# Probabilities turned by VectorE block transposes and DMAs across partitions, in place of TensorE transposes

## The reference: what is computed

```python
# first branch: 16 heads of 64, causal
q, k, v = einsum('bse,ef->bsf', xn, W_qkv)           # (8, 512, 3, 16, 64)
q, k = rotary_embedding(q), rotary_embedding(k)
scores = einsum('bqhd,bkhd->bhqk', q, k) / 8
weights = softmax(where(tril, scores, -1e9))
attn = einsum('bhqk,bkhd->bqhd', weights, v).reshape(8, 512, 1024) @ W_out
# second branch: 16 heads of 8, not causal, then a mixture of 8 experts
q, k, v = xn @ Wq + bq, xn @ Wk + bk, xn @ Wv + bv
ctx = softmax(q k^T / sqrt(8)) v
y = xn + layernorm(ctx @ Wo + bo)
p = softmax(y @ Wg + bg);  top 2 of 8 experts, weighted
ffn = y + layernorm(sum of the two picked (y @ We[e] + bexp[e]) * p[e])
out = x + attn + ffn
```

## Time and profile before

| what | before |
|---|---|
| median of three runs | 1271.35 us (1267.77 to 1273.54) |
| profiled execution: its span | 1270.3 us |
| instructions | 25325 |
| busy PE / DVE / ACT / POOL | 1159.3 / 928.0 / 892.0 / 811.5 us |
| mean granted TensorE clock | 0.978 |
| DMA traffic | 42.87 MB, 34 GB/s |

### The profile page before, as it was taken

One profiled execution on the slowest core, in us unless ns is written; L12 is line 12 of the kernel. 1 busy time (PEld: TensorE's weight loads), 2 busy tenths in 40 slices (PEclk: granted clock), 3 DMA queues, 4 the chain that ended last, 5 costly groups with the idle time before them and its releaser, 6 DMA issues.

```text
span 1270.3 us, 25325 instructions
## 1 busy us (share of the span) xinstructions
PE 1159.3 (91%) x9387; PEld 741.3 (58%) x9387; DVE 928.0 (73%) x2336; ACT 892.0 (70%) x1841; POOL 811.5 (64%) x730
## 2 busy tenths in 40 slices
PE   4779999999999999999999999999999999899986
PEld 3355565655666565655656556665656556575655
DVE  7666487885878857896687848787687866778546
ACT  3567867487766868578775887668776796748860
POOL 3655774577855767568864778467675587645760
PEclk8799999999999999999999999999999999999998
DMA  4000100011000110001100011001000011000000
GB/s 144 34 34 18 43 35 17 26 39 38 34 18 26 51 43 26 18 26 59 39 13 35 26 43 42 18 26 51 34 29 24 25 35 51 18 17 34 34 18 9
DMA packets 34110, 42.87 MB, mean 34 GB/s; under 512 B 5694, under 2 KB 17216, under 8 KB 33988
## 3 DMA queue, kind: packets, MB, share of 16 engines
q1 hardware_dynamic: 30516, 38.31, 8.2%
q10 hardware_dynamic: 3472, 2.95, 0.8%
HBM read 5.60 MB, written 2.10 MB: 6 GB/s over the span
## 4 chain that ended last, share of the span: by engine, by line
PE 59%; DVE 17%; ACT 14%; issue 4%; POOL 4%; DMA 1%; SPq 0%; ACTq 0%; DVEq 0%; POOLq 0%
PE work L1319 7%; PE work L1233 7%; PE work L1334 6%; PE work L1346 6%; PE work L1235 6%; PE work L1234 6%; PE work L1396 5%; DVE fnmax L1071 5%; ACT fpt L884 5%; PE work L1362 4%; ACT pn L926 4%; DVE work L1193 3%; PE work L1371 3%; PE work L1386 3%; ACT pt L938 2%
## 5 line engine op out<-in xcount | busy, mean ns | idle before, releaser
L926 ACT ACTIVATE pn<-work,nmax 128x512 f32<-128x512 f32 (+3 forms) x512 | 265.3, 534 | 119.9 <-DVE nmax L1193 119.4
L785 POOL TENSOR_TENSOR raw<-raw,cos_t 128x512 f32<-128x512 f32 x128 | 163.8, 1280 | 284.9 <-DMA swapped<-raw 269.7
L1071 DVE TENSOR_REDUCE fnmax<-work 128x2 f32<-128x1024 f32 x256 | 302.0, 1219 | 47.0 <-PE work L1371 45.8
L1193 DVE CUSTOM_DVE_ANT_0 work<-work,causal 128x512 f32<-128x512 f32 (+3 forms) x512 | 236.1, 520 | 95.5 <-PE work L1319 94.7
L884 ACT ACTIVATE fpt<-work 128x1024 f32<-128x1024 f32 x256 | 252.4, 1029 | 52.7 <-PE work L1386 51.4
L1334 PE MATMUL work<-consts,pn 128*128 128x128 f32 x1280 | 172.6, 277 | 7.0 <-DVE fnmax L1071 4.0
L789 POOL TENSOR_TENSOR raw<-raw,swapped 128x512 f32<-128x512 f32 x128 | 163.7, 1279 | 10.0
L1334 PEld LDWEIGHTS work<-consts,pn 128*128 128x128 f32 x1280 | 141.1, 141 | 42.7 <-DVE fnmax L1071 13.0
L800 POOL TENSOR_TENSOR qk_l<-raw,qk_h 128x512 fp32r<-128x512 f32 x128 | 163.3, 1282 | 2.8
L786 POOL TENSOR_TENSOR swapped<-swapped,sin_t 128x512 f32<-128x512 f32 x128 | 163.7, 1279 | 0.0
L938 ACT COPY pt<-work 128x1024 f32<-128x1024 f32 x128 | 130.4, 1019 | 42.6 <-PE work L1334 42.1
(11 more groups left out here) (161 smaller groups left out, 2140.1 us busy)
## 6 DMA issues: line engine op xcount, KB each, us to landing
swapped<-raw SPq DMA_DIRECT2D x256, 128.0 KB, 2.0
x_in<-in_L_attn_x_dram SPq DMA_DIRECT2D x8, 256.0 KB, 3.4
out_dram<-x_in SPq DMA_DIRECT2D x7, 256.0 KB, 2.2
fpt<-in_L_attn_W_qkv_dram ACTq DMA_DIRECT2D x3, 512.0 KB, 5.9
pt<-in_L_ffn_We_dram ACTq DMA_DIRECT2D x1, 512.0 KB, 7.2
wout<-in_L_attn_W_out_dram ACTq DMA_DIRECT2D x1, 512.0 KB, 8.4
out_dram<-x_in SPq DMA_DIRECT2D x2, 128.0 KB, 1.8
pt<-in_rope_dram ACTq DMA_DIRECT2D x1, 192.0 KB, 6.5
```

What stands on the lines that cost most here:

```text
L785: nc.gpsimd.tensor_tensor(raw[:, n % 3], raw[:, n % 3], cos_t[:], ALU.mult)
L926: ins = nc.scalar.activation(pn[:, h, PN_AT[j]:PN_AT[j] + n], bank_of(("sc", b, c, unit), h)[:, at:at + n], ACT.Exp, scale=-1.0, bias=nmax ...
L1071: nc.vector.tensor_reduce(fnmax[:, j, 2 * r:2 * r + 2, 0:1], bank_of(("fsm", b, g, j), 2 * r, 2).rearrange("p (f n) -> p f n", f=2), AX.X, ...
L1193: ins = nc.vector.tensor_tensor_reduce(out=scores, in0=scores, in1=causal[:, S - n:S], scale=-1.0 / math.sqrt(DH), scalar=3.0e38, op0=ALU.add,
```

## The change

What it does, part by part:

1. The transposes `tp`, `tq` and their copies `tpe`, `tqe` go. A new kind `tr` on DVE (line 1588 of the changed kernel) transposes 32 x 32 blocks of `pn` in place, three instructions a chunk: 128 x 8 x 128, 128 x 8 x 128 and 128 x 8 x 64 elements, one for each unit of `exp`. A new kind `shuf` on SP's queue (line 1140) then sends, with four DMAs a chunk, each from 32 partitions of `pn` to all 128 of `pt`, 128 x 640 elements (327,680 bytes), so that blocks which belong to one key land on one partition. `pn` becomes double, `pt` single; `exp` waits for the `shuf` of two chunks ago, `shuf` waits for the third `tr` and for the `pv` of the chunk before, `pv` waits for its `shuf`.
2. A 32 x 32 block transpose would leave keys in another order than tiles of 128 need. So POOL's `hi` and `lo` write keys (k = 1) with a step of 32 elements, the mask is put in the same order once, `exp` writes runs of 32, `pv` reads runs of 32, in five groups of four matmuls instead of four (the same 1280 columns), and the query tiles stand in reverse order in `rT` and `ao`.
3. Second branch: `fqk` is made once a batch with the plain weights (6 matmuls of 128 x 512 instead of 24), `fqkh` and `fqkl` with 2 instructions a batch instead of 8; a new kind `fdup` on SP (line 1147), three DMAs a group, spreads the parts over the strips. `fsub` writes to a buffer of its own, `fqm`, and also waits for the `fst` of the group before.
4. `fan` writes straight to `l_wide` (and so waits for the `div` of the chunk before). At the start a few transposes, casts and small DMAs are fewer, and raw loads stand in `pn` instead of `pt`.
5. The tables START, SHIFT, FIRST, LAST become one table PLACE with a place number for each instance; the PSUM table changes too.

```diff
```diff
+TILES_OF = {3: 0, 2: 4, 0: 7, 1: 8}
+UNIT_TILES = [slice(0, 4), slice(4, 8), slice(8, 10)]
+PT_N = T * (T + 1) // 2
+QUADS = P // STRIP
...
-START = {
-    "turn": [-465.460287],
...
+PLACE = {
+    "xT": [
+        [0],
...
-        pn = sb("pn", [P, 2, PT_N])
-        pt = sb("pt", [P, 2, 2, PT_N])
-        l_rows = sb("l_rows", [P, S])
+        pn = sb("pn", [P, 2, QUADS, 2, PT_N, STRIP])
+        pt = sb("pt", [P, QUADS, 2, PT_N, STRIP])
-        fqk = sb("fqk", [P, 2, 2, S], F32R)
+        fqn = sb("fqn", [P, 4, S], F32R)
+        fqs = sb("fqs", [P, 2, 2, S], F32R)
+        fqm = sb("fqm", [P, S], F32R)
...
+        def landed(kind, *key):
+
+            sems, per, dmas = (fdup_done, G, 3) if kind == "fdup" else (shuf_done, NC, QUADS)
+            n = key[0] * per + key[1]
+            return (sems[n % 2], 16 * dmas * (n // 2 + 1)) if n >= 0 else (begun, 1)
 
...
+                elif kind == "shuf":
+                    c = x_[2]
+                    wait(sp, after("tr", b, c, 2))
+                    wait(sp, after("pv", *ring(1, b, c, NC)))
+                    for a in range(QUADS):
+                        sp.dma_start(pt[:, a].rearrange("p h n r -> p (h n r)"),
+                                     pn[a * STRIP:(a + 1) * STRIP, c % 2].rearrange("p c h n r -> p c (h n r)")).then_inc(shuf_done[c % 2], 16)
+                elif kind == "fdup":
+                    g = x_[2]
+                    wait(sp, after("fqkl", b))
+                    wait(sp, after("fst", *ring(2, b, g, G), T - 1))
+                    for c, pair in ((1, slice(0, 4, 2)), (2, slice(1, 3)), (3, slice(0, 4, 3))):
+                        sp.dma_start(fqs[c:P:4, g % 2].bitcast(F32), fqn[g * STRIP:(g + 1) * STRIP, pair].bitcast(F32))                            .then_inc(fdup_done[g % 2], 16)
...
+            def turned(a, k):
+                return a.rearrange("p (t c r) -> p t r c", c=QUADS, r=STRIP) if k == 1 else a
+            def plain(a, k):
+                return a.rearrange("p (t r c) -> p t r c", c=QUADS, r=STRIP) if k == 1 else a
...
-                    nc.gpsimd.tensor_copy(qk_h[:, c % 2, k], raw[:, n % 3]).then_inc(done["hi"], 1)
+                    nc.gpsimd.tensor_copy(turned(qk_h[:, c % 2, k], k), plain(raw[:, n % 3], k)).then_inc(done["hi"], 1)
...
-                    nc.gpsimd.tensor_tensor(qk_l[:, c % 2, k], raw[:, n % 3], qk_h[:, c % 2, k].bitcast(F32),
-                                            ALU.subtract).then_inc(done["lo"], 1)
+                    nc.gpsimd.tensor_tensor(turned(qk_l[:, c % 2, k], k), plain(raw[:, n % 3], k),
+                                            turned(qk_h[:, c % 2, k].bitcast(F32), k), ALU.subtract).then_inc(done["lo"], 1)
...
                 elif kind == "fqkh":
-                    g = x_[2]
-                    wait(act, after("fst", *ring(2, b, g, G), T - 1))
+                    wait(act, after("fqk", b))
...
+                    for k in range(2):
+                        ins = nc.scalar.activation(fqn[:, 2 * k], bank_of(("fqk", b), k), ACT.Identity, bias=qk_bias[:, k:k + 1])
...
-                        wait(act, after("tp", *ring(1, b, c, NC), 1))
-                        wait(act, after("tq", *ring(1, b, c, NC)))
+                        wait(act, landed("shuf", *ring(2, b, c, NC)))
+                        if b == 0 and c < 2:
+                            for kind_ in LOADED:
+                                wait(act, after(kind_, 0))
...
-                        ins = nc.scalar.activation(pn[:, h, PN_AT[j]:PN_AT[j] + n], bank_of(("sc", b, c, unit), h)[:, at:at + n],
+                        tiles = slice(TILES_OF[j], TILES_OF[j] + j + 1)
+                        ins = nc.scalar.activation(pn[:, c % 2, :, h, tiles].rearrange("p c i r -> p i c r"),
+                                                   bank_of(("sc", b, c, unit), h)[:, at:at + n].rearrange("p (i c r) -> p i c r", r=STRIP, c=QUADS),
...
-                elif kind == "tpe":
-                    c, unit = x_[2:]
...
-                        wait(act, after("pv", *ring(2, b, c, NC)))
-                    nc.scalar.copy(pt[:, c % 2, :, unit * S:(unit + 1) * S],
...
                     wait(act, after("inv", b, c))
-                    wait(act, after("rT", *ring(1, b, c, NC)))
-                    nc.scalar.copy(l_rows[:].rearrange("p (t h n) -> p t h n", t=T, h=2),
+                    wait(act, after("div", *ring(1, b, c, NC)))
+                    nc.scalar.copy(l_wide[:].rearrange("p (t h n) -> p t h n", t=T, h=2),
...
                 elif kind == "fqkl":
-                    g = x_[2]
-                    wait(dve, after("fqkh", b, g))
+                    wait(dve, after("fqkh", b))
...
-                    nc.vector.tensor_tensor(fqk[:, g % 2, 0], bank_of(("fmT", b, g)), fqk[:, g % 2, 0].bitcast(F32),
-                                            ALU.add).then_inc(done["fsub"], 1)
+                    wait(dve, after("fst", *ring(1, b, g, G), T - 1))
+                    nc.vector.tensor_tensor(fqm[:], bank_of(("fmT", b, g)), fqs[:, g % 2, 0].bitcast(F32), ALU.add).then_inc(done["fsub"], 1)
...
-                elif kind == "tqe":
-                    c = x_[2]
-                    wait(dve, after("tq", b, c))
...
+                elif kind == "tr":
+                    c, unit = x_[2:]
+                    wait(dve, after("exp", b, c, unit, 0), after("exp", b, c, unit, 1))
+                    blocks = pn[:, c % 2, :, :, UNIT_TILES[unit]].rearrange("p c h n r -> p c h (n r)")
+                    nc.vector.transpose(blocks, blocks).then_inc(done["tr"], 1)
...
-                    g = x_[2]
-                    if g == 0:
-                        wait(pe, after("xl", b))
-                        if b == 0:
-                            wait(pe, after("strl", 0))
+                    wait(pe, after("xl", b))
+                    if b == 0:
+                        wait(pe, after("strl", 0))
                     for k in range(2):
-                        wh = strips_h[:, k, g * GH:(g + 1) * GH].rearrange("p h c -> p (h c)")
-                        wl = strips_l[:, k, g * GH:(g + 1) * GH].rearrange("p h c -> p (h c)")
-                        ins = split3(bank_of(x_, k), wh, wl, xt_h[:, b % 2], xt_l[:, b % 2])
+                        ins = split3(bank_of(x_, k), wqk_h[:, k], wqk_l[:, k], xt_h[:, b % 2], xt_l[:, b % 2])
...
-                elif kind in ("tp", "tq"):
-                    c, unit = x_[2], 2 if kind == "tq" else x_[3]
...
-                                                                  pn[:, h, from_:from_ + P], ident)
-                    ins.then_inc(done[kind], 1)
                 elif kind == "pv":
                     c = x_[2]
-                    wait(pe, after("tpe", b, c, 0), after("tpe", b, c, 1))
-                    wait(pe, after("tqe", b, c))
+                    wait(pe, landed("shuf", b, c))
                     if c == 0:
                         wait(pe, after("vc", b, T - 1))
-                    for i in range(T):
+                    for i, js in ((0, (3, 2, 1)), (0, (0,)), (1, (3, 2, 1)), (2, (3, 2)), (3, (3,))):
+                        first, at = TILES_OF[js[0]] + i, (T - 1 - js[0]) * P
                         for a in range(0, 2 * DH, STRIP):
                             h = a // DH
-                            ins = nc.tensor.matmul(psum[a:a + STRIP, i * P:S], v[:, i, 2 * c + h, a % DH:a % DH + STRIP],
-                                                   pt[:, c % 2, h, PT_AT[i]:PT_AT[i] + S - i * P],
-                                                   start=i == 0, stop=i == T - 1, tile_position=(0, a))
+                            moving = pt[:, :, h, first:first + 4 * len(js) - 3:4] if len(js) > 1 else pt[:, :, h, first:first + 1]
+                            ins = nc.tensor.matmul(psum[a:a + STRIP, at:at + len(js) * P], v[:, i, 2 * c + h, a % DH:a % DH + STRIP],
+                                                   moving.rearrange("p a j r -> p j a r"),
+                                                   start=(i, js[0]) == (0, 3), stop=i == T - 1, tile_position=(0, a), skip_group_check=True)
...
-                        wait(pe, after("fqkl", b, g))
+                        wait(pe, landed("fdup", b, g))
```

1108 lines of the change are left out of this document (643 added, 465 removed), and 277 rows, old and new, of tables (FIRST, LAST, LAST_PSUM, PLACE).

## The result

The changed kernel takes 1419.84 us, the median of four runs (1409.35 to 1421.89), beside 1272.44 us of the kernel before on the same chip (1267.77 to 1276.6). The ratio is 1.114, with a 95% interval of 1.109 to 1.119: 11% slower. The prediction said 1206 us, a range of 1140 to 1285, and 0.17 for slower.

What follows compares the result with a forecast made beforehand. DVE was to become the busiest engine: 128.9 us busy, 7.8 idle and 5.75 stalls make 142.45 a batch, 8.15 below 150.6; eight batches give span 1205.1, median 1206 us. Range 1140 to 1285.

Steps and rivals of the forecast that it cites:

- Busy times: Per batch after the change: PE 118.0 us, DVE 128.9 and busiest, ScalarE 89.8, GpSimd 110.9.
- a sign of being wrong: In the profile after: the forecast is wrong if PE is still the busiest engine; PE was expected at about 960 us.
- waits for the shuffle over 14 us a batch: In the profile after: waits for shuf above 14 us a batch would show the forecast wrong; some 6 were expected.
- The shuffle: From third block transpose to landing: 7.5 us, between 5.8 and 9.3; with 2.35 for pv, 5.75 us of stalls a batch.
- The half-rate end, 9.3: Shuffle DMAs reading 32 partitions at half rate: 7.1 + 2.2 = 9.3 us, 14.6 of stalls; rival at 8.2 to 9.3, chance 15%.
- The shuffle lands later still, slower than before: Rival: the wait at pv stops PE, then DVE's division, eight times a batch; 1309 us at 10 us, 1408 at 12; chance 12%.
- the period without stalls: Per batch: DVE busy 128.9 us plus the busiest engine's present idle time, 7.8, gives 136.7.
- the prediction's largest saving: On PE: the 160 transposes go, 172.6 us over 8 batches, 21.6 a batch.
- GpSimd and merged fqk: Strided hi and lo add 7.6 us a batch, covered by DVE; 18 fewer fqk matmuls save PE 4.1 a batch.
- the swaps: On SP behind the shuffles: each lands 3.6 to 7 us later; GpSimd, 110.9 of 141 us busy, can take it.
- The cover of each chunk: DVE work between a chunk's third block transpose and division: 6.9, 7.4, 9.5, 10, 10.5, 11, 14 and over 16 us.

Runs made afterwards that it cites:

- e2: Quarter-row kernel: the changed kernel with each shuffled row cut from 2560 to 640 bytes, as many DMAs; 1240.9 us, ratio 0.973.
- e8: The kernel with quarter rows, with block transposes of only the first 32 columns of each run; 1217.5 us.
- b2: The kernel before without PE's transposes of the probabilities and their ACT and DVE copies from the second batch on; 1298.5 us, ratio 1.020.
- e13: The kernel with quarter rows plus eight useless 128x512 matmuls in front of each product with v; 1311.4 us.
- e3: The changed kernel with GpSimd's hi and lo for keys written without the step of 32 elements; 1412.6 us, ratio 1.111.
- b1: The kernel before with fqk, fqkh and fqkl of groups 1 to 3 left out from the second batch on; 1270.0 us, ratio 0.997.
- half rows: The changed kernel with each shuffled row cut from 2560 to 1280 bytes; 1254.9 us, ratio 0.987.
- b4: b2 with PE's 160 transposes a batch still executed, on a constant, uncopied and waiting for no exp; 1262.2 us, ratio 0.992.
- m1: A program of only the shuffle's DMAs, varying source partitions, queues and row sizes; 8.6 us a round as in the change, 5.0 from every fourth partition.
- m2: The DMA-only program with other source and destination partitions; rounds of 8.7, 8.0, 5.1, 8.0, 12.5 and 8.2 us.

## Why the prediction was wrong, point by point

- **Busy times: right, but for PE.** Block transposes 1.231 and 0.683 us, (156.9 + 43.7)/8 = 25.1 us a batch against 24.3; DVE 1034.0 us against 1045; ScalarE 742.4 against 892.0 - 8 x 20.7 = 726; GpSimd's `hi` and `lo` (30.6 + 16.7)/8 = 5.9 us a batch against 7.6. PE was to have 960 and has 1110.0, still the most of all engines. The prediction named that as a sign of being wrong, and another, waits for the shuffle over 14 us a batch, is met too: 113.1/8 = 14.1 on PE alone.
- **The shuffle: the step that failed most.** Of the 214 us between 1206 and 1420 it makes 133: the sum had 8 x 5.75 = 46 us of stalls, and with quarter rows 179 go away. The wait was foreseen; two terms of it were mis-sized. The sum took 7.5 us from the third block transpose to the landing, the middle of 5.8 and 9.3. It is 9.7 in the kernel and 8.6 a round alone; with 9.7 the prediction's own covers give 17.0 us of stalls a batch, 136 in all, 90 more than it had. And it took 2.35 us for the product behind the wait, which at the clock that a stop leaves takes 3.3 on average (211.9/64). The half-rate end, 9.3, was the right one: rows of swaps that read every second of all partitions could not tell a DMA from 32 neighbours, and the middle of two mechanisms is neither of them.
- **The rival that came true.** "The shuffle lands later still, slower than before" gave 1309 us for 10 us, with the chance of 12%. Its mechanism is there: the product is waited for, then the division. Its price was too low by 110 us.
- **The other step: the period without stalls, 82 us.** The sum took "Busy DVE 128.9, idle of the busiest engine as now, 7.8". The quarter-row kernel has almost no stall at the product (0.7 us) and takes 1241 us, where the same sum gives 1270.3 - 8 x 13.9 = 1159. Idle time as now was assumed without a reason: PE's rises from 111.0 to 198.3 us, and DVE is idle for 202.9. e8 shows that DVE does not bound: 110 us of its work are worth 23. b2 shows for the lists of the kernel before that the removal of the transposes' PE work, the prediction's largest saving (21.6 us a batch, which also counts the row whole), is worth nothing or less: the clock falls from 0.978 to 0.906. The quarter-row kernel has the same low clock, 0.903, but that the clock makes its 82 us is not shown; filling it in one lump (e13) did not give them back, and the cause there stays open. These 82 us are most of the 110 by which the late-shuffle rival was too low; the product at 1.2 GHz is part of the rest.
- **GpSimd and merged fqk: right to leave GpSimd out; the swaps stay open.** e3 moves the ratio by 0.004, and b1 gives 0.3% for three quarters of `fqk` without any price. The prediction had 4.1 us a batch for that on PE; it, too, came to nothing.
- **The cover of each chunk: near.** The lists were counted to give 6.9 to over 16 us between transpose and division. The product itself starts 7.6 us after the issue in the median, and half rows, 5.4 us long, cost 14 us in all.

## What to carry to other kernels

A wait that a change adds has a threshold: find the work that stands beside it in the lists, and price the unknown length by each mechanism apart, not by their middle. Before you price removed work on the busiest engine at its busy time, ask what the clock and the lists make of the holes, and whether its rows overlap; leaving the work out without replacing it costs one run and tells. A single buffer that closes a circle (this product, next transfer, next product) may not be hidden by moving the product later; here it was not.

## What the runs showed of the hardware

- Taking 151 us of matmuls (by their row) and their copies out made a kernel slower by 2.0% and lowered the granted TensorE clock from 0.978 to 0.906 (b2); 150 us of useless ones in the same places, still without the copies, brought 0.980 and a time 0.8% under the kernel before (b4).
- Four DMAs of 327,680 bytes each from SBUF to SBUF take 5.0 to 5.2 us a round when each reads partitions over all 128, 8.0 from within 64, 8.6 from 32 neighbours, and 12.5 when each reads all 128 and writes 32 neighbours (m1, m2).
- The four DMAs of a shuffle are issued in 5.1 us, not in 4 x 0.72: the first two take 0.6 us each and the last two 1.9 each. With quarter rows (e2), or alone from every fourth partition (m1), each takes some 0.6 and the four 2.5.
- GpSimd's cast that writes with a step of 128 bytes takes 1.09 us instead of 0.61, (108.4 - 77.8)/64 more, and the subtraction that reads and writes so 1.54 instead of 1.28; without the steps (e3) both are back at their old means.
